# A tower of front convolutions, attention, slices, GRU and experts on one core: both front convolutions on row tiles of TensorE, loads and setup in another order

## The reference

```python
h = jnp.stack([x[:, :D // 2], x[:, D // 2:]], axis=1)              # (64, 2, 4096)
h = _maxpool(relu(_bn(_conv1d(h, w1, b1, 1, 1), ...)), 8)         # (64, 16, 512)
h = _maxpool(relu(_bn(_conv1d(h, w2, b2, 1, 1), ...)), 4)         # (64, 64, 128)
h = _self_attn(h, wq, bq, wk, bk, wv, bv, gamma)                  # out = gamma * v attn + h
h = _bn(_conv1d(h, w3, b3, 2, 1), ...)                            # (64, 128, 64)
h = h + window_attention(layernorm(h))
h = h + slice_attention(layernorm(h))
h = h + bidirectional_gru(layernorm(h))
h = h + top2_of_8_experts(layernorm(h))
```

## Time and profile before

| | us |
|---|---|
| median of 3 runs | 1342.02 |
| lowest, highest | 1342.01, 1344.54 |
| the profiled execution | 1346.97 |
| its span, first to last instruction | 1345.1 |
| mean granted clock of TensorE | 0.962 of full |
| PE, DVE, ACT, POOL busy | 1232.2, 869.1, 815.5, 620.6 |

### The profile page before, as it was taken

How to read it: one execution, slowest core, us unless ns; L and a number is a source line. 1 busy time by engine, 2 the same in 40 slices (tenths; PEclk the granted TensorE clock), 3 DMA queues, 4 the chain that set the end, 5 groups by cost and what they waited for, 6 DMA issues and landing times.

```text
span 1345.1 us, 42753 instructions
## 1 busy us (share of the span) xinstructions
PE 1232.2 (92%) x15668; PEld 827.9 (62%) x15668; DVE 869.1 (65%) x2952; ACT 815.5 (61%) x2513; POOL 620.6 (46%) x938
## 2 busy tenths in 40 slices
PE   6998997999999997999999998899999999879997
PEld 2445764555555555777777777666666664456665
DVE  3775445777777776787788786555555554746664
ACT  2994545888888884445455455555555556635553
POOL 5001245677676774365556555333333332335555
PEclk9997996999999998999999999899999999969999
DMA  8400000000000000000000000000000000000000
GB/s 229 100 0 1 1 1 1 1 0 0 0 0 0 0 1 1 3 0 0 0 0 0 0 0 2 2 1 0 0 0 0 0 0 1 1 1 19 16 16 17
DMA packets 10318, 14.00 MB, mean 10 GB/s; under 512 B 9232, under 2 KB 9360, under 8 KB 9744
## 3 DMA queue, kind: packets, MB, share of 16 engines
q1 hardware_dynamic: 10256, 13.15, 4.0%
HBM read 11.05 MB, written 2.10 MB: 10 GB/s over the span
## 4 chain that ended last, share of the span: by engine, by line
PE 59%; issue 14%; DVE 10%; POOL 10%; ACT 5%; POOLq 1%; DMA 1%; DVEq 0%; ACTq 0%; SPq 0%
PE bank L1333 7%; POOL big L534 6%; PE bank L1672 5%; PE bank L1690 5%; PE bank L145 5%; PE bank L1328 4%; PE bank L1034 3%; PE bank L1357 3%; PE bank L1061 2%; PE bank L164 2%; PE bank L359 2%; PE bank L1437 2%; PE bank L1102 2%; PE bank L1112 2%; PE bank L1026 2%
## 5 line engine op out<-in xcount | busy, mean ns | idle before, releaser
L534 POOL TENSOR_TENSOR big<-big 128x512 f32<-128x512 f32 x128 | 133.2, 1041 | 59.8 <-DVE big L729 59.8
L698 ACT ACTIVATE big<-big 128x128 f32<-128x128 f32 x384 | 148.9, 394 | 1.3 <-DVE big L741 1.3
L1405 POOL TENSOR_TENSOR big<-g_a,g_b 64x64 f32 x128 | 40.4, 315 | 185.1 <-DVE g_a L1395 185.1
L940 POOL TENSOR_TENSOR big<-big 128x512 f32<-128x512 f32 x64 | 65.7, 1047 | 118.9 <-DVE big L1210 118.9
L641 PEld LDWEIGHTS bank<-cst,big 128*128 128x128 f32 x512 | 57.4, 142 | 73.4 <-issue 61.4
L1726 ACT ACTIVATE big<-bank 128x512 f32<-128x512 f32 x128 | 66.2, 602 | 51.9 <-PE bank L1672 51.9
L741 DVE CUSTOM_DVE_ANT_0 big<-bank,cst 128x128 f32<-128x128 f32 x384 | 88.7, 287 | 13.7 <-issue 13.7
L1593 POOL TENSOR_TENSOR big<-big 128x512 f32<-128x512 f32 x48 | 61.0, 1270 | 76.2 <-DVE big L1796 73.6
L1372 ACT ACTIVATE g_r<-bank,g_bias 128x64 f32<-128x64 f32 x128 | 40.2, 314 | 89.1 <-PE bank L1333 89.0
L595 PE MATMUL bank<-big 32*128 32x512 f32 x256 | 77.9, 660 | 17.8 <-POOL big L528 10.3
L1386 DVE SCALAR_TENSOR_TENSOR g_t<-bank,cst,g_r 128x64 f32<-128x64 f32 x128 | 36.3, 284 | 85.7 <-ACT g_r L1372 85.7
(11 more groups left out here) (269 smaller groups left out, 3356.5 us busy)
## 6 DMA issues: line engine op xcount, KB each, us to landing
big<-x_dram SPq DMA_DIRECT2D x12, 512.0 KB, 8.2
cst<-consts_dram SPq DMA_DIRECT2D x1, 3364.5 KB, 22.4
out_dram<-h SPq DMA_DIRECT2D x8, 256.0 KB, 2.6
cst<-consts_dram SPq DMA_DIRECT2D x3, 256.0 KB
cst<-consts_dram SPq DMA_DIRECT2D x1, 279.5 KB, 2.9
g_ih_exchanged<-consts_dram SPq DMA_DIRECT2D x2, 96.0 KB, 8.1
a_proj_padded<-consts_dram SPq DMA_DIRECT2D x8, 2.0 KB
cst<-consts_dram SPq DMA_DIRECT2D x8, 2.0 KB
```

The costliest lines, as they stand in the source:

```text
L534: nc.gpsimd.tensor_tensor(P, P, a_rs[t % 4].unsqueeze(2).to_broadcast([128, 4, 128]), ALU.mult).then_inc(a_n_r, 1)
L698: m = nc.scalar.activation(P, raw, ACT.Exp, bias=a_mx[tb % 4][:, k:k + 1], scale=-1.0, accum_out=a_sm[tb % 4][:, k:k + 1])
```

## The change

x now lies on partitions 0 to 47 (eight samples, 3 taps by 2 channels by 8) and 64 to 111 (the other eight), written by six DMAs of 16 rows for two groups, and twelve of half length for the first. Conv1 uses one set of weights on both 64-row tiles: two matmuls of 48 rows into two banks, for 512 positions of all 16 samples. So a half h (8 in all) has four such pairs; each pair is followed by one max of 1024 columns, the first of a half after ACT has copied its sums to SBUF. Conv2 reads `h1`, one padded buffer for a group, at shifts 0, 1 and 2: for each tap four matmuls of 32 rows, on four 32-row tiles, sum up in four banks, 12 matmuls for a group. Its weights `w2q` come by twelve DMAs. ACT does one relu of 512 columns for a group instead of twelve. DVE takes max2 in two instructions of 1024 columns instead of four of 512. The loop is written out. The setup stands elsewhere: the packing of wq and wk after half 4, the f rows after half 7, the middle steps between max2 of groups 5 and 6 (two on DVE, two copies on ACT, one product on POOL), conv2 of group 7 behind the first products, and the a_bv product, the middle product, a_pb, the mixed and the centre steps in the first slot of 1b, where the general wait for `h2_ready` is gone and only the edges of `h3g` are cleared. SP's order is constants up to w1, w1s (two DMAs), x of groups 0 and 1 (twelve), w2q (twelve), x of groups 2 and 3 (six), the large constants, the experts' loads, then x of the next groups. The core of the diff:

```diff
-    xin = [big1[0:96, 0:LEN], big1[0:96, LEN:2 * LEN]]
+    xin = [big1[:, 0:LEN], big1[:, LEN:2 * LEN]]
...
-    h1raw = [big2[:, 512 * k:512 * (k + 1)] for k in range(2)]
-    h2raw = [big2[:, 1024 + 512 * k:1024 + 512 * (k + 1)] for k in range(2)]
-    taps = big2[0:96, 2048:2048 + 8 * 512].rearrange("p (k n) -> p k n", k=8)
+    one = sb("one", [128, 1])
+    h1raw = [big2[:, 1024 * k:1024 * (k + 1)].rearrange("p (g n) -> p g n", g=2) for k in range(2)]
+    h2raw = [big2[:, 6152 + 512 * k:6152 + 512 * (k + 1)] for k in range(2)]
+    h1 = big2[:, 3072:3072 + 4 * 514].rearrange("p (k n) -> p k n", k=4)
+    c1_copy = big2[:, 5128:5128 + 1024]
+    w2q = cst[:, ON["w1"][0]:ON["w1"][0] + 384]
...
+    def conv1_banks(k):
+        return T(0, 2 * (k % 2), 2)
...
+        def conv1(h, k):
+            i, q = h // 2, 4 * (h % 2) + k
+            if q == 0:
+                pe.wait_ge(x_loaded[i % 2], 96 * (i // 2 + 1))
+            elif i == 0 and q == 4:
+                pe.wait_ge(x_half, 18 * 16)
+            if k == 2:
+                pe.wait_ge(c1_copied, h + 1)
+            elif k == 3:
+                pe.wait_ge(c1_max, 4 * h + 2)
+            elif h:
+                pe.wait_ge(c1_max, 4 * h - 1 + k)
+            for g in range(2):
+                r = slice(64 * g, 64 * g + 48)
+                m = nc.tensor.matmul(conv1_banks(k)[:, 512 * g:512 * (g + 1)], w1s[r, :], xin[i % 2][r, 512 * q:512 * (q + 1)],
+                                     start=True, stop=True)
+            m.then_inc(c1_sum, 1)
+        def conv2(j):
+            pe.wait_ge(h1_ready, j + 1)
+            if j:
+                pe.wait_ge(c2_max, 2 * j)
+            for t in range(3):
+                for p in range(4):
+                    r = slice(32 * p, 32 * p + 32)
+                    m = nc.tensor.matmul(T(1, p), w2q[r, 128 * t:128 * (t + 1)], h1[r, j % 4, t:t + 512], start=(t == 0), stop=(t == 2))
+            m.then_inc(c2_sum, 1)
+        pe.wait_ge(w_scaled, 2)
+        for h in range(HALVES):
+            if h < JA:
+                for k in range(3):
+                    conv1(h, k)
+            if h == 2:
+                pe.wait_ge(w_scaled, 3)
+            if h >= 2:
+                conv2(h - 2)
+            if h < JA:
+                conv1(h, 3)
+            elif h == JA:
+                pe.wait_ge(c1_max, 4 * JA)
                 pe.wait_ge(loaded, 16)
                 setup3_first_pe(pe)
...
+        def max1(h, k):
+            i, q = h // 2, 4 * (h % 2) + k
+            if k:
+                v.wait_ge(c1_sum, 4 * h + k + 1)
             else:
+                v.wait_ge(c1_copied, h + 1)
+            if i >= 2 and q == 0:
+                v.wait_ge(h1_ready, 2 * i - 2)
+            sums = conv1_banks(k) if k else c1_copy
+            nc.vector.tensor_reduce(h1raw[i % 2][:, :, 64 * q:64 * (q + 1)], sums.rearrange("p (g n k) -> p g n k", g=2, k=8),
+                                    X, ALU.max).then_inc(c1_max, 1)
+        def max2(j):
+            v.wait_ge(c2_sum, j + 1)
+            if j >= 2:
+                v.wait_ge(h2_ready, j - 1)
+            for k in range(2):
+                nc.vector.tensor_reduce(h2raw[j % 2][:, 256 * k:256 * (k + 1)], T(1, 2 * k, 2).rearrange("p (n k) -> p n k", k=4),
+                                        X, ALU.max).then_inc(c2_max, 1)
+        def scale2():
+            v.wait_ge(bn_rs, 3)
+            v.wait_ge(x_half, 18 * 16)
+            nc.vector.tensor_tensor(bn_s[:, 16:80], bn_s[:, 16:80], c("bn_g", 16, 80), ALU.mult).then_inc(bn_scale, 1)
+            v.wait_ge(bn_scale, 4)
+            w2v = w2q.rearrange("p (a c) -> p a c", c=64)
+            nc.vector.tensor_tensor(w2v, w2v, bn_s[:, 16:80].unsqueeze(1).to_broadcast([128, 6, 64]), ALU.mult).then_inc(w_scaled, 1)
+        for h in range(HALVES + 1):
+            if h >= 3:
+                max2(h - 3)
+            if h < JA:
+                for k in range(4):
+                    max1(h, k)
+            if h == 1:
+                scale2()
+            elif h == 4:
+                v.wait_ge(loaded, 16)
+                v.wait_ge(b_w, 1)
+                for to, name, at in ((0, "wq", 0), (32, "wq", 192), (64, "wk", 0), (96, "wk", 64)):
+                    nc.vector.tensor_copy(wqk[:, to:to + 8], c(name, at, at + 8)).then_inc(b_w, 1)
+                nc.vector.tensor_scalar(a_bqs[:, :], c("a_bq"), -HD ** -0.5, None, ALU.mult).then_inc(a_setup, 1)
+                nc.vector.tensor_reduce(a_m4[:, :], c("a_mask").rearrange("p (g j) -> p j g", j=4), X, ALU.add).then_inc(a_setup, 1)
+                nc.vector.tensor_scalar(c("a_bias"), c("a_bias"), -1.0, None, ALU.mult).then_inc(a_setup, 1)
+                nc.vector.tensor_scalar(gbv[:, :], c("bv"), c("gamma"), None, ALU.mult)
+            elif h == JA - 1:
+                setup3_rows_dve(v)
+            elif h == JA:
                 setup3_middle_dve(v)
...
+        def copy1(h):
+            act.wait_ge(c1_sum, 4 * h + 1)
+            if h:
+                act.wait_ge(c1_max, 4 * h - 3)
+            nc.scalar.copy(c1_copy, conv1_banks(0)).then_inc(c1_copied, 1)
+        def relu1(j):
+            act.wait_ge(c1_max, 8 * (j // 2) + 8)
+            if j >= 4:
+                act.wait_ge(c2_sum, j - 3)
+            nc.scalar.activation(h1[:, j % 4, 1:513], h1raw[j // 2 % 2][:, j % 2, :], ACT.Relu, bias=bn_t[:, 0:1]).then_inc(h1_ready, 1)
+        def relu2(j):
+            act.wait_ge(c2_max, 2 * j + 2)
+            nc.scalar.activation(h2all[:, 4 * j:4 * j + 4, :], h2raw[j % 2].rearrange("p (r n) -> p r n", r=4), ACT.Relu,
+                                 bias=bn_t[:, 1:2]).then_inc(h2_ready, 1)
         act.wait_ge(bn_shift, 2)
         act.wait_ge(pads_zero, 2)
+        for h in range(HALVES + 1):
+            if h < JA:
+                copy1(h)
+            if h >= 2 and h % 2 == 0 and h <= JA:
+                relu1(h - 2)
+                relu1(h - 1)
+            if h == JA + 1:
+                setup3_copies_act(act)
+            if h >= 3:
+                relu2(h - 3)
...
-        pool.wait_ge(h2_ready, JA + 2)
...
+                pe.wait_ge(h2_ready, (s + 1) // 2 + 1)
...
+            if s == -1:
+                pe.wait_ge(c2_max, 2 * JA)
+                nc.tensor.matmul(bank(5)[:, 0:128], c("a_bv"), c("a_p"), start=True, stop=True).then_inc(a_pb_ps, 1)
+                setup3_middle_pe(pe)
...
-        v.wait_ge(h2_ready, JA + 2)
-        for k in range(2):
-            nc.vector.memset(h3g[k], 0.0).then_inc(pads_zero, 1)
...
+            if s == -1:
+                for k in range(2):
+                    nc.vector.memset(h3g[k][:, :, 0:130:129], 0.0).then_inc(pads_zero, 1)
+                v.wait_ge(a_pb_ps, 1)
+                nc.vector.tensor_tensor(a_pb[:, :], bank(5)[:, 0:128], c("a_bp"), ALU.add).then_inc(a_pb_r, 1)
+                setup3_mixed_dve(v)
+                setup7_centre_dve(v)
...
+    def setup3_copies_act(act):
+        act.wait_ge(f_pe, 1)
+        nc.scalar.copy(fGT, T(0, 0)[0:64, 0:64]).then_inc(f_dve, 1)
+        nc.scalar.copy(fV, T(0, 1)[0:64, :]).then_inc(f_dve, 1)
...
+        for r, k, at in slice_logits():
+            nc.vector.scalar_tensor_tensor(heads(fX[r, at:at + 512]), c("f_bslice")[r].unsqueeze(1).to_broadcast([64, 8, 64]), 1.0 / C,
+                                           heads(T(0, k)[r, :]), ALU.mult, ALU.add).then_inc(f_zero, 1)
+    def setup3_middle_pool(pool):
+        pool.wait_ge(f_zero, 5)
+        pool.wait_ge(m_made, MADE7)
+        bs = fX[:, :].rearrange("p (s h c) -> p s h c", s=2, c=64)
+        nc.gpsimd.tensor_tensor(bs, bs, fti[:, :].unsqueeze(1).unsqueeze(3).to_broadcast([128, 2, 8, 64]), ALU.mult).then_inc(f_dve, 1)
...
-        for r in (slice(0, 64), slice(64, 128)):
-            for k in range(8):
-                q = slice(64 * k, 64 * k + 64)
+        for k in range(8):
+            q = slice(64 * k, 64 * k + 64)
+            for r in (slice(0, 64), slice(64, 128)):
                 nc.tensor.matmul(T(0, 0)[r, q], fFT[:, q], fM[:, q], start=True, stop=True)
                 m = nc.tensor.matmul(T(0, 1)[r, q], fFT[:, q], fV[:, q], start=True, stop=True)
...
+            front = AT["w1"][0]
+            sp.dma_start(cst[:, 0:front], consts[:, 0:front]).then_inc(conv_loaded, 16)
+            o = front
+            for g in range(2):
+                sp.dma_start(w1s[64 * g:64 * g + 48, :],
+                             consts[0:96, o + 128 * g:o + 128 * g + 128].rearrange("(k b) n -> k b n", b=16)[:, 8 * g:8 * g + 8, :]).then_inc(conv_loaded, 16)
+            def x_load(i, a, b, to):
+                for g in range(2):
+                    for t in range(3):
+                        sp.dma_start(xin[i % 2][64 * g + 16 * t:64 * g + 16 * t + 16, a:b],
+                                     xp[i, :, a + t:b + t].rearrange("(c s) n -> c s n", c=2)[:, 8 * g:8 * g + 8, :]).then_inc(to, 16)
+            x_load(0, 0, LEN // 2, x_loaded[0])
+            x_load(0, LEN // 2, LEN, x_half)
```

(92 more changed lines are left out.)

101 lines of the change are left out of this document (22 added, 79 removed).

## The result

The changed kernel took 1416.37 us (median of 4 runs, 1414.69 to 1419.79) against 1342.29 (4 runs): the ratio is 1.0551 with an interval of 1.0528 to 1.0574, that is +74.1 us. Its profiled execution took 1419.79 us, with a span of 1417.9 (before 1345.1) and a mean granted clock of 0.948. The prediction said 1406, in a range of 1318 to 1424, slower with 0.72.

The account below looks back on a forecast made before the run. PE bounds the front; after the change, x loads on two DMA engines: last x at 136.5 us plus a 45 us tail, +63.9, less 0.3 for setup products, +63.6 on the 1342.02 median: 1406 us, range 1318 to 1424.

Parts of the forecast that it names:

- (a): Rival on the x loads: wide, 16 or 8 engines at 210 GB/s; 1324 us, or 1312 without waiting for x2; chance 0.23.
- (b): Rival on the x loads: sixteen engines, but slower for so few partitions, 105 GB/s; 1344 us; chance 0.07.
- Outer count 2, two engines: x loads in the front: the source's outer count of 2 lets only two DMA engines carry each load; chance 0.62.
- 26.9 GB/s an engine: x loads: each of the two engines moves 26.9 GB/s, so a group of 1.57 MB takes 29.2 us, four 117 us.
- Rival (c): x loads: two engines at only 13.1 GB/s each, so 117 us becomes 240; 1529 us; chance 0.05.
- The ledger of the loads, last x at 136.5: Front's DMA queues: 3.5 start + 117 x + 8 constants + 7.1 experts + 0.5 + 0.5 = 136.5 us.
- The tail, 45 us: From the last x landing through halves 6 and 7 and the setup to the next stage's first maximum: 45 us.
- The mark: Start of the next stage's first DVE maximum, taken as the front's end: forecast 181.5 us instead of 117.6, +63.9.
- PE 6.2 us, period 7.4 us a half: Front's steady halves, engines alone: PE needs 6.2 us instead of 10.3, the next half starts at 7.4; 23 us saved.
- Rival (d): Front's row tiles don't overlap as cheaply, with wide loads: 17.2 us of PE a half, some 1390 us; chance 0.03.
- Rival (e): Clock falls in steady halves from two PE gaps of 0.7 us: 12.2 us of PE a half; no chance given.

Follow-up runs that it names:

- e1: The changed kernel with x rows reordered by the host so each x load's source has an outer count of 16: 1348.05 us, 1.0038 to the kernel before.
- e9: The kernel before with only the source of x padded, so its outer count is 2 and two DMA engines carry each x load: 1412.78 us, ratio 1.0548.
- e11: e8 with the f rows moved behind max2(5) and the first setup products behind conv2(6): 1319.59 us, 0.9824 to the kernel before.
- e3: The changed kernel with x rows reordered so each x load's source has an outer count of 8: 1352.54 us, 1.0074 to the kernel before.
- e6: e1 with x in loads of 48 rows, two DMAs for two groups instead of six, w1 laid out to match: 1336.62 us, 0.9974 to the kernel before.
- e8: e6 with f rows behind half 5, setup products before conv2(6), middle steps behind max2(6), one w2 DMA, x2 before the large constants: 1322.32 us, 0.9861 to before.

## Why the prediction was right, point by point

The mechanism was the one forecast, and 1416.4 lies 10 us above the 1406. The range on record, 1318 to 1424, was wide enough to hold rivals (a) and (b) as well; but the narrower range given for two engines alone, 1393 to 1420, holds the result too.

**Outer count 2, two engines.** Right, and shown in both directions (e1, e9) and by the completions at 2, 4, 8 and 16 (568, 628, 748, 988). The Trainium skill's rule ("DMA: Bandwidth & Descriptors", section on why a DMA increments its semaphore by 16) gives these counts, and six for each w1s load. The packets agree to the last one.

**26.9 GB/s an engine.** Measured where x flows alone: 16 KB in 0.61 us (the 0.66 above is the average, with the slow ones beside other loads), 53 GB/s for two, the last pair of groups in 29.7 us instead of 29.2. Rival (c), 13.1 GB/s an engine, is out: in e9 two engines write into 32 partitions at 0.67 us a packet, so that figure of the earlier trace rows is what sixteen engines get into them together, not what an engine can do.

**The ledger of the loads, last x at 136.5.** The term that was most off: 143.9, 7.4 late. The packets' own times in the trace take it apart.

| | predicted, us | measured, us |
|---|---|---|
| first packet of x1 | 33.2 | 35.7 |
| x1 | 29.2 | 36.8 |
| from x1's landing to x2's first packet (constants, experts) | 15.6 | 8.5 |
| x2 | 29.2 | 33.2 |
| x3 | 29.2 | 29.7 |

x1 landed at 72.5 instead of 62.4. Up to 46 us the constants ran beside it (226 to 318 GB/s in the slices from 32 to 44), and x1's packets then took up to 1.53 us, most of them 0.9 or more, instead of 0.61; a few were slow again beside the experts' loads. But the constants did not run on x1's two engines at that time: 112 of their 128 rows, eight for each of fourteen engines, had started by 46 us, and the other sixteen came only from 68.6 to 79.9, as x1 ended. So loads slowed x1 although they had other engines, which my sum had at nothing, and it cost most of the 7.6 us. What then stood between x1 and x2 was 7.1 us shorter than my sum, since most of the experts' packets had been moved meanwhile. That these two errors nearly cancel is luck.

**The tail, 45 us.** 47.5. The steps up to conv2(6) came as predicted (first matmuls 5.49 for 5.2, conv2(6) at 25.05 for 24.3 and 5.50 long for 5.3). Where it failed: conv2(7) was put at 2.7 us with an escape clause, "if the second cold spell does not end, conv2(7) costs 2.6 more". It took 4.96, after 4.06 us of idle PE. The mark is 7.4 + 2.5 = 9.9 us over the forecast, which is +73.9 against +63.9. The clearing of h3g, the pair of 1.01 us for the middle product (1.01 again) and the small order change of the last products made nothing visible. Behind the mark I had allowed -0.3 us, for the last setup products; the span grew by 1.1 us less than the mark moved, of which I did not take the parts.

**PE 6.2 us, period 7.4 us a half.** The steady half, seen in e1's full-clock stretch and in e11, is 7.60 (maxima at 55.45, 63.05 and 70.64 in e11), DVE's wait inside it 0.72 for 0.6. Rounds on four 32-row tiles take 2.86 / 3 = 0.95 us, mine 0.86; the estimate by the Trainium skill's factor ("TensorE: Matmul & The Clock Gate", Part 3) was 1.12, and the row lies between. Rival (d), tiles that don't overlap, is out: a round would be 3.43.

**Rival (e), the clock in steady halves.** Out: 1.00 granted from 75 to 95 us of e1, with PE's two gaps a half (1.53 at most).

**Rivals (a) and (b), wide loads.** e1 is (b): I had 1344 from 105 GB/s for sixteen partitions, and 1348 was measured with 131. (a), 1312 to 1324, needs 210 GB/s into sixteen partitions, which no run showed; e3 and e1 both end at some 111 to 133. So had the source been written with one count, this change would have been no gain (+0.4%): the faster engines wait for x, and the tail is longer.

## What to carry to other kernels

Before splitting one load into several with fewer rows, work out from the packets how many DMA engines each will use and how many partitions it writes: the outer counts of source and destination set the first, and few partitions can cap the rate even when all sixteen engines work (131 GB/s in e1). When the engines of a stage get faster, look first at what feeds it; here the loads had to be rebuilt (e6) and reordered (e8) before the faster convolutions were worth anything. A setup step put between two groups costs its own time and, if it stops PE for long (3.68 us and more in these runs), half clock for the next group too; place it beside the work of another engine, and check which pause it makes.
